# Closing work of layer 0 inside layer 1's first attention block, with moved constants, scattered DMAs and expert groups

## What is computed

```python
xn = _layernorm(x)
x = x + L0_attn(xn) + L0_switchhead(xn)      # softmax attention, and 8 heads with 8 experts each
xn = _layernorm(x)
x = x + L1_attn(xn) + L1_moe(xn)

# L1_attn: positive random features, 16 heads of 8, 64 features
k_prime = ratio * exp(proj k - |k|^2/2 - max over tokens and features) + 1e-4
q_prime = ratio * exp(proj q - |q|^2/2 - max over features) + 1e-4
out = (q_prime @ (k_prime^T v)) / clip(q_prime @ sum(k_prime), 1e-2) @ Wo.T + bo

# L1_moe
logits = xf @ gate_w + gate_b;  top 2 of 8, softmax of the two -> combine
out = sum_e combine_e * (gelu(xf @ w1[e] + b1[e]) @ w2[e] + b2[e]) + gelu(xf @ ws1 + bs1) @ ws2 + bs2
```

## Time and profile before

| | us |
|---|---|
| median of 3 runs | 3363.51 |
| lowest and highest | 3355.54, 3365.3 |
| the profiled execution, its own time | 3354.0 |
| its span in the profile | 3352.2 |

### The profile page before, as it was taken

One profiled execution on the slowest core, in us unless ns is written; L12 is line 12 of the kernel. 1 busy time (PEld: TensorE's weight loads), 2 busy tenths in 40 slices (PEclk: granted clock), 3 DMA queues, 4 the chain that ended last, 5 costly groups with the idle time before them and its releaser, 6 DMA issues. The chain is left out here.

```text
span 3352.2 us, 51674 instructions
## 1 busy us (share of the span) xinstructions
PE 3032.0 (90%) x17486; PEld 2092.8 (62%) x17486; DVE 2384.9 (71%) x4419; ACT 1612.1 (48%) x3262; POOL 1826.2 (54%) x2258
## 2 busy tenths in 40 slices
PE   2999999999999999999999999999999246798967
PEld 1567666666666666666666666666666234566644
DVE  6888888888888888888888888888885330424242
ACT  1355555555555555555555555555555112262612
POOL 1466666666666666666666666666664244011052
PEclk7899999999999999999999999999999577899988
DMA  4000001100100011010101100110000211133211
GB/s 153 20 21 21 21 27 36 31 21 22 34 27 21 21 30 30 22 34 28 32 21 31 30 21 22 34 33 21 21 21 8 50 39 59 61 92 117 64 51 29
DMA packets 143160, 123.47 MB, mean 37 GB/s; under 512 B 28458, under 2 KB 123956, under 8 KB 142900
## 3 DMA queue, kind: packets, MB, share of 16 engines
q1 hardware_dynamic: 130884, 88.88, 9.4%
q0 software_dynamic: 9712, 28.93, 2.8%
q10 hardware_dynamic: 2304, 2.36, 0.4%
HBM read 91.56 MB, written 28.57 MB: 36 GB/s over the span
## 5 line engine op out<-in xcount | busy, mean ns | idle before, releaser
L1167 DVE TENSOR_REDUCE m_peaks<-m_ring 128x1 f32<-128x512 f32 x1024 | 641.5, 682 | 116.9 <-PE m_ring L266 111.2
L925 ACT ACTIVATE m_expA<-m_ring 128x512 f32<-128x512 f32 x1024 | 538.9, 601 | 367.4 <-PE m_sums L354 176.8
L816 POOL TENSOR_TENSOR m_vprod<-m_vprod 128x512 f32<-128x512 f32 x256 | 355.4, 1388 | 497.0 <-DVE m_vprod L1180 495.3
L825 POOL TENSOR_TENSOR m_oprod<-m_oprod 128x512 f32<-128x512 f32 x256 | 328.5, 1283 | 282.3 <-DVE m_oprod L1249 282.3
L317 PE MATMUL m_ring<-m_probT,m_vs 128*128 128x256 f32 x2048 | 466.9, 381 | 0.0
L896 ACT ACTIVATE m_prob<-m_ring,m_negs 128x512 f32<-128x512 f32 x512 | 347.4, 684 | 240.4 <-DVE m_negs L1214 240.4
L317 PEld LDWEIGHTS m_ring<-m_probT,m_vs 128*128 128x128 f32 x2048 | 384.2, 190 | 79.7 <-issue 27.7
L1208 DVE TENSOR_REDUCE m_negs<-m_ring 128x1 f32<-128x512 f32 x512 | 340.6, 685 | 92.4 <-PE m_ring L94 92.0
L1249 DVE TENSOR_TENSOR m_oprod<-m_ring,m_go 128x512 f32<-128x512 f32 x512 | 341.6, 686 | 58.8 <-PE m_ring L94 55.3
L1180 DVE TENSOR_TENSOR m_vprod<-m_ring,m_gate 128x512 f32<-128x512 f32 x512 | 336.9, 684 | 42.0 <-POOL m_vs L818 21.5
L906 ACT ACTIVATE m_probT<-m_ring 128x512 f32<-128x512 f32 x512 | 285.4, 597 | 56.4 <-PE m_ring L305 52.6
(11 more groups left out here) (288 smaller groups left out, 5483.4 us busy)
## 6 DMA issues: line engine op xcount, KB each, us to landing
m_wraw<-in_v_w SPq DMA_DIRECT2D x32, 512.0 KB, 4.0
m_qf<-q_dram SPq DMA_DIRECT2D x128, 128.0 KB, 2.6
m_wraw<-in_o_w SPq DMA_DIRECT2D x32, 512.0 KB, 4.2
q_dram<-m_kf SPq DMA_DIRECT2D x24, 256.0 KB, 3.0
m_xg<-listed SPq DMA_DIRECT2D x39, 128.0 KB
answers<-m_yg SPq DMA_DIRECT2D x39, 128.0 KB, 1.8
listed<-m_oprod SPq DMA_DIRECT2D x9, 512.0 KB, 7.1
sums_dram<-m_sumsT ACTq DMA_DIRECT2D x128, 18.0 KB
```

The source lines that it names most:

```text
L816: vchain(pool.tensor_tensor(vprod[:, 0:512], vprod[:, 0:512], vprod[:, 512:1024], ALU.add))
L825: ochain(pool.tensor_tensor(op[:, 0:512], op[:, 0:512], op[:, 512:1024], ALU.add))
L925: act.activation(expA[hh][:, c * 512:(c + 1) * 512], ring.home["scT", n, k, hh, c][:, :], ACT.Exp)\
L1167: v.tensor_reduce(peaks[:, t, hh, c:c + 1], ring.home["peaks", n, t, hh, c][:, :], AX.X, ALU.max)\
```

## The change

- **Closing of layer 0's last batch.** The products, sums, norm, transposes and routing of batch 3 and the routing of batch 2's last part move out of `layer0` into slots 0 to 13 of block 0 of layer 1. The counting of places moves from slot 1 to slots 13 to 16 in four pieces (`mark_choices`, `keep_places`, `scan_tiles`, `rank_tokens`). SyncE's 33 DMAs of sums and denominators stand at the head of layer 1.
- **Constants.** The 15 loads are issued in layer 0, at step 29 of 32, into memory that layer 0 no longer uses then. The lower parts of the weights are made on VectorE; the parts of x in pieces (ScalarE 512 columns, GpSimd 256).
- **Scattered DMAs.** The rows are sent in slots 16 to 34 (from block 0's end through block 1) instead of 1 to 16; the answers are fetched four at a time in slots 1 to 16 of block 3. In both stretches GpSimd waits for named sums of VectorE (`let_vector`).
- **Groups.** They run in slots 36 to 54 instead of 19 to 53.
- **Units.** Two in block 0, three in block 1, three in block 3. The bias product is four more matmuls at the end of each `output`, into the same tile; `bias` and `add_biases` are gone.

```diff
-UNIT_SLOTS = {2 + 3 * s + part: (s, part) for s in range(4) for part in range(3)}
-FETCH_SLOTS, ANSWER_SLOTS = {1 + 2 * q: q for q in range(8)}, {3 + 2 * q: q for q in range(8)}
+UNIT_SLOTS = {0: {2 + 2 * k: (k // 3, k % 3) for k in range(6)},
+              1: {2 + 5 * s + part: (2 + s, part) for s in range(3) for part in range(3)},
+              B - 1: {2 + 4 * s + part: (5 + s, part) for s in range(3) for part in range(3)}}
+FIRST_SENT, FIRST_GROUP = SLOTS - 2, 2 * SLOTS
+ANSWER_SLOTS = {3 + 2 * q: q for q in range(8)}
...
 # layer0, tensor (the lists of the other engines lose their part in the same way)
-                routing(B - 2)
-                project_out(B - 1, 0)
-                project_out(B - 1, 1)
-                turn_xo(B - 1, 0)
-                turn_xo(B - 1, 1)
-                routing(B - 1)
...
 # layer0, sync
+                    if i == N0 - 3:
+                        sp.wait_ge(xn_turned, 2 * B)
+                        sp.wait_ge(gates_ready, 2 * B)
+                        load_layer1()
...
 def group_slots():
-    first, last = SLOTS + 1, 3 * SLOTS
+    first, last = FIRST_GROUP, 3 * SLOTS + 1
...
 # main1, tensor: output(s)
+                    pe.wait_ge(cT_kept, s + 1)
                     for t in range(4):
                         for k in range(HT):
-                            last = pe.matmul(ps[:, t * P:(t + 1) * P], hT[:, k, t * P:(t + 1) * P], w2[:, k, :],
-                                             start=(k == 0), stop=(k == HT - 1))
+                            pe.matmul(ps[:, t * P:(t + 1) * P], hT[:, k, t * P:(t + 1) * P], w2[:, k, :],
+                                      start=(k == 0), stop=False)
+                        last = pe.matmul(ps[:, t * P:(t + 1) * P], cT[:, t * P:(t + 1) * P], b2, start=False, stop=True)
...
 # main1, tensor: block 0
+                        if b == 0 and u == 5:
+                            project_out(0)
+                            project_out(1)
+                        if b == 0 and u == 9:
+                            turn_xo(0)
+                            turn_xo(1)
+                        if b == 0 and u == 11:
+                            routing(B - 1)
+                        if b == 0 and u == 14:
+                            count_places()
...
 # main1, gpsimd
+                def let_vector(b, u):
+                    s, part = UNIT_SLOTS.get(b, {}).get(u - 1, (None, None))
+                    if part == 2:
+                        pool.wait_ge(x_mixed, s + 1)
+                    if u == 0:
+                        pool.wait_ge(o_divided, 2 * b)
+                    if u == 1:
+                        pool.wait_ge(v_kept, b + 1)
+                    if u == 15:
+                        pool.wait_ge(kvw_made, b + 1)
+                    if u == 16:
+                        pool.wait_ge(o_divided, 2 * b + 1)
...
-                        if b == 0 and 1 <= u < 17:
-                            send_rows(2 * u - 2)
-                            send_rows(2 * u - 1)
-                        if b == 0 and u == 17:
+                        if FIRST_SENT <= n < FIRST_GROUP - 1:
+                            let_vector(b, u)
+                            slots_of = FIRST_GROUP - 1 - FIRST_SENT
+                            for k in range(2 * NT * (n - FIRST_SENT) // slots_of, 2 * NT * (n + 1 - FIRST_SENT) // slots_of):
+                                send_row(k)
+                        if n == FIRST_GROUP - 1:
                             for j in range(NW):
                                 fetch_weights(j)
...
-                        if b == B - 1 and u in FETCH_SLOTS:
-                            fetch_answers(FETCH_SLOTS[u])
+                        if b == B - 1 and 1 <= u < 17:
+                            let_vector(b, u)
+                            fetch_answers((u - 1) // 2, (u - 1) % 2)
```

More of the change, by code:

```diff
@@ L1 @@
+from collections import namedtuple
 from contextlib import ExitStack
+import math
 import numpy as np
@@ L1676, in main1 @@
-        over = early[:, 1536:1536 + NG * EM].rearrange("p (j e) -> p j e", e=EM)
-        full = early[:, 1536 + NG * EM:1536 + NG * EM + 128].rearrange("p (e k) -> p e k", k=16)
+        full = early[:, 768:896].rearrange("p (e k) -> p e k", k=16)
+        scan = [later[:, 384 * k:384 * (k + 1)].rearrange("p (t e) -> p t e", e=EM) for k in range(2)]
+        before = later[:, 768:1024].rearrange("p (t e) -> p t e", e=EM)
+        over = later[:, 0:NG * EM].rearrange("p (j e) -> p j e", e=EM)
+        last_rows = late.oT[:, :].rearrange("p (t d) -> p t d", t=TPB)
@@ L2013, in _ @@
                             project_in(b, 1, qT_made, qT_kept)
-                            turn_combine(b, 0)
-                            if b == 0:
-                                count_places()
-                        s, part = unit_part(b, u)
+                        if b == 0 and u == 0:
+                            routing(B - 2)
+                        s, part = UNIT_SLOTS.get(b, {}).get(u, (None, None))
                         if part == 2:
@@ new lines, in add_late_attn, with token_moments @@
+                def add_late_attn(q):
+                    xt = x[:, NT - TPB + 4 * q:NT - TPB + 4 * q + 4, :].rearrange("p t d -> p (t d)")
+                    v.wait_ge(late.out_made, 2 * B - 1 + q)
+                    v.tensor_tensor(xt, xt, ring.home["late attn", q][:, 0:512], ALU.add).then_inc(late.attn_added, 1)
+                def token_moments():
+                    v.wait_ge(late.attn_added, 2 * B)
+                    for t in range(NT - TPB, NT):
+                        last = v.bn_stats(late.st["bn"][:, t, :], x[:, t, :])
+                    rk(last)
@@ new lines, in choose_experts @@
+                def choose_experts(b):
+                    v.wait_ge(late.lg_kept, b + 1)
+                    one, other = top2(v, rk, late.lg[:, :, :], late.tmp, order[:, :],
+                                      [choice[:, q, b * TPB:(b + 1) * TPB] for q in range(2)])
+                    rk(v.tensor_tensor(one, one, other, ALU.add))
+                    v.tensor_tensor(late.lg[:, :, :], late.lg[:, :, :], spread(late.tmp["first"], 8), ALU.subtract)\
+                        .then_inc(late.lg_ready, 1)
@@ new lines, in mark_choices @@
+                def mark_choices():
+                    v.wait_ge(late.o_divided, 2 * B)
+                    for k in range(2):
+                        v.memset(scan[k][:, 0:16, :], 0.0)
+                        v.memset(cum[k][:, 0:4], 0.0)
+                    for q in range(2):
+                        last = v.tensor_tensor(marks[q], order[:, :].unsqueeze(1).to_broadcast([P, NT, EM]),
+                                               spread(choice[:, q, :], EM), ALU.is_equal)
+                    rk(last)
+                    v.tensor_tensor(marks[2], marks[0], marks[1], ALU.add).then_inc(consts_ready, 1)
@@ L2103, in rank_tokens @@
                                        ALU.add))
+                def rank_tokens():
+                    v.wait_ge(late.mixed, B)
+                    for q in range(2):
+                        rk(v.tensor_tensor(scan[1][:, 16:48, :], combine[:, :, 0:EM], marks[q], ALU.mult))
+                        rk(v.tensor_reduce(shares[:, q, :], scan[1][:, 16:48, :], AX.X, ALU.add))
                     for q in range(2):
@@ L2412, in lower_x, with divide_o @@
                         return
-                    pool.wait_ge(x_upper, b + 1)
-                    lower(pool, xh[b % 2][:, 1, :], xnT[:, b * T:(b + 1) * T], xh[b % 2][:, 0, :]).then_inc(x_split, 1)
+                    for c in range(2):
+                        pool.wait_ge(x_upper, 2 * b + c + 1)
+                        for cols in (slice(512 * c + 256 * k, 512 * c + 256 * (k + 1)) for k in range(2)):
+                            last = lower(pool, xh[b % 2][:, 1, cols], xnT[:, b * T + cols.start:b * T + cols.stop],
+                                         xh[b % 2][:, 0, cols])
+                        last.then_inc(x_split, 1)
+                def divide_o(q):
+                    if q == 0:
+                        pool.wait_ge(late.o_loaded, 512 * B)
+                    heads = slice(8 * q, 8 * q + 8)
+                    pool.tensor_tensor(late.oT[:, :].rearrange("p (u h) -> p h u", h=H0)[:, heads, :], late.o_in[:, heads, :],
+                                       late.rden_in[:, heads, :], ALU.mult).then_inc(late.o_divided, 1)
                 def square_k(b):
```

396 lines of the change are left out of this document (231 added, 165 removed).

## The result

The changed kernel takes 3327.4 us, median of 4 runs (3327.0 to 3332.1); the kernel before took 3363.2, timed beside it. The ratio is 0.990, 95% interval 0.9885 to 0.9914: 36 us less, where I had said 73 less. The profiled execution spans 3330.2 us against 3352.2 before: only 22 less, because it is the slowest of the changed kernel's four, while the one before was 9.5 us under its median.

The account below looks back on a forecast made before the run. Layer 0 is bound by TensorE, so gains lie in the last 750 us, where the bound differs by stage. Terms -64 - 77 + 93 - 24 = -72 us give span 3280, forecast 3290 us, range 3235 to 3347.

Parts of the forecast that it names:

- Start of layer 1, minus 64: Between layer 0 and layer 1: TensorE starts at about 2612 us instead of 2676, bounds minus 61 to minus 65.
- Block 0, 130 us: Block 0 of layer 1: falls from 207 us to 130 with two units and the closing added, minus 77.
- base of 128: Blocks 0 and 3: attention with four units takes 128 us once the visible holes are taken out.
- Rival 4: Block 0: the closing costs more than it hides, plus 20 to 26 us, about 3313; chance 0.11.
- Blocks 1 and 2, unstalled: Blocks 1 and 2 without holes from sends: 121 us for attention with three units, 254 us with the added groups.
- base of 148: Block 2 before the change, taken as 148 us; 16 more groups at 5.6 us each were added to it.
- Rival 3: Block 2: groups become bound by their transfers, slower than before, 3375 us; chance 0.05.
- The sends' holes in block 1, 24 us: Block 1: three bursts of sends cost 8 us each despite the waits, between 0 and 64 us.
- The fetches' holes in block 3, 18 us: Block 3: holes beside the fetches shrink from 35 us to about 18, bounds 0 and 35.
- at most eights: Block 3: after the first 16 fetches run free in slots 1 to 4, later ones come in eights at most.
- rival 1: Blocks 1 and 3: the burst itself is the trouble, 57 us more, about 3347, half 3320; chance 0.2, whole or half.
- the 26 us: Block 0, first burst: a VectorE sum with SBUF and PSUM inputs waits 26 us beside GpSimd's indirect DMAs.

Follow-up runs that it names:

- e7: The kernel before without its 64 sends and 64 fetches (output lacks the experts' part): 3235.0 us, one execution.
- e2: The changed kernel without its 64 sends, 64 fetches and the waits on VectorE's sums: 3240.1 us, ratio 0.966 to the kernel before.
- e4: Separate program, no part of the model: a chain of small TensorE, VectorE and ScalarE steps; 50 steps take 85.0 us alone, 116.4 beside 32 gathers in a row.

## Why the prediction was wrong

I forecast 3290 us and measured 3327.4; as spans of the profiled execution, in which the sum was made, 3280 and 3330.2. By the forecast's own steps, in the order of the sum:

- *Start of layer 1, minus 64: nearly right.* TensorE starts at 2615.20 instead of my 2612. GpSimd's last sum of layer 0 ends at 2612.22, 2.9 us later than before, and from there it takes 3.0, as said. Plus 3 us.

```profile
2611.77 0.45 POOL L864 TENSOR_TENSOR k_x<-k_x,m_oprod 128x128 f32<-128x128 f32 x1
...
2615.20 0.77 PE L98 MATMUL m_ring<-m_xh,m_wh 128*128 128x512 f32 x1 [7.74 <-POOL m_xh L88]
```

- *Block 0, 130 us: right within its bounds.* It took 138.4 (133.7 by the squares, which start 4.7 us after TensorE's first product; here it is counted from that product). Two errors hide each other. My base of 128 for four units is 112 in e7, and the 14 us for closing and ranking are more like 38, if that base holds in block 0 too: 138.4 less 100, which remain of the base when two units at 5 us and the biases' 2 go. That is just inside my bounds of 5 to 40. Rival 4 is right in its direction, by 8 us instead of 20.
- *Blocks 1 and 2, unstalled: near in the sum, block 2 by luck.* Without DMAs block 1 takes 112.8 (I had 121). Block 2 with the groups that spill into block 3's first slot, some 13 us, takes 257 (I had 254). That hides two errors. My base of 148 came from a window that began at 3041 us, 12 us into the block: by the squares block 2 took 162.6 before, with 21 groups, and 37 groups made it 243.7, so 16 more cost 81 us or 5.1 each, not 5.6. Rival 3 (transfers) doesn't appear: the window of block 2 shows TensorE busy 204 of 244 us at 116 GB/s, none of TensorE's waits there is released by `m_wg` or `m_xg`, and the largest, 26 us in all, are for the gelu.
- *The sends' holes in block 1, 24 us: the first step that failed.* The sends cost 41.3 (e2). I had taken three short bursts; they ran in rows of 17, 14 and 17.
- *The fetches' holes in block 3, 18 us: the step that failed most.* The fetches cost 46.5, hardly less than the 48.8 before. I had counted holes of 35 there, because I took everything that was no visible hole for the attention's own time. The base of 128 us was itself stretched by 16 (e7). The argument "at most eights" was wrong as well: the fetches wait for the last group's answers, and the first one starts 17 us into the block. From then on GpSimd is behind its slots and runs in three rows of 16, before it gets down to 8 and 4:

```profile
3168.80 0.99 POOL L2604 DMA_INDIRECT m_rows<-answers,m_place  x1 [15.54 <-DMA answers<-m_yg]
```

Together 87.8 us where I had 42: 46 of the 50 us by which the span missed. The other five terms, the start, block 0, block 1, block 2 and block 3 without their holes, add up to 4 (3 + 8 - 8 + 3 - 2).

So it was rival 1, whose half I had at 3320 and whose whole at 3347: the row itself is the trouble. I gave it 0.2. The two rows on which it rested, TensorE's stepping in the earlier trace rows and the end of the second hole 15 us after the last send, were the right evidence. What I set against it, that VectorE's sums start right behind the last send, fits both theories, since everything starts again there. And one row that spoke plainly against my reading stood in the trace of the kernel before, right above the peaks of the earlier trace rows: the row of sends begins at 2695.53, and ten microseconds into it VectorE runs just such a sum, of x and PSUM (L2227), 2.6 us after its product has ended and 30 us before the row has. What matters is how long the row has been going on, not what VectorE reads:

```profile
2705.42 0.69 DVE L2227 TENSOR_TENSOR k_x<-k_x,m_ring 128x512 f32<-128x512 f32 x1 [5.58 <-remote]
2706.14 2.36 DVE L2154 TENSOR_REDUCE m_peaks<-m_ring 128x16 f32<-128x1024 f32 x2
```

The Trainium skill, SBUF — State Buffer, section "SBUF: two separate sides", is not contradicted after all. By it the unit's sum, which reads one tile of SBUF, should not be blocked, and e4 shows the same standstill with no tile in SBUF read by VectorE. I was wrong to read the 26 us as a trace that disagrees with the rule.

What stays open: what it is in the indirect DMAs that delays TensorE's signals and instructions. Bytes are not it (rows of 128 B cost the same), nor the direction (scatters too), nor, it seems, DMAs of GpSimd as such (32 plain ones, 0.53 us apart, cost nothing; they last 16 us in all, as long as 13 indirect ones, and 12 of those cost 5). The Trainium skill, Runtime: NRT & Kernel Launch, section "Instruction fetch mechanics", says that each engine's instructions are brought in by DMA into a small buffer. Engines that first run on and then get an instruction every 1.40 us would look as if that came late. But the traces list these transfers, as queues of kind "instruction", and they speak against a late refill. In e4, in 85 us of TensorE at full speed (545 to 630), and then in the 26 us in which it steps (648 to 674.5), the queues are:

```profile
q8 instruction: 4, 0.07, 0.3%
q14 instruction: 1, 0.01, 0.0%
...
q0 software_dynamic: 672, 1.38, 17.6%
```

While TensorE steps, no instruction transfer is under way at all. How instructions get on from the buffer no run shows. Another rival is untested: the recording of the profile. In the phase without semaphores the trace holds 19 of the 50 counts of VectorE beside the row, and all 50 without it, so whatever the row holds up, records go missing with it. No run here was timed against the same kernel without recording, so I can't say that the recording has no part in the cost. Open too is why block 3 of the changed kernel, one unit lighter and without its first slot, takes 119 us in e2 where e7's takes 112; the rows show the granted clock at 0.87 against 0.94, and not why it is lower.

And where the 65 us of the earlier start went: without DMAs, from e7 to e2, the start gives 64.8 and block 1 37.5 (its groups left), block 0 takes 10.6 (closing in, two units and the ranking's wait out), block 2 takes 78.4 and block 3 20.6, of which some 13 are groups. That is plus 7 in all. The start less block 0 gives 54, and the groups take 54 (78.4 + 13 - 37.5): by these sums what the overlap of the closing saved was paid for by the groups that now run with nothing of the attention beside them. No run has the closing moved alone.

## What to carry to other kernels

Before a wait on one engine's progress is used to pace another, look at what the engines do that the wait doesn't protect: if all of them stop, and one with all its inputs shows idle time put down to issue, the cause is no operand conflict. Space indirect DMAs on GpSimd in short lots, here four to six with a mean distance of at least 1.5 us, for example by waiting until each four have landed; one pause between long rows doesn't do it, and a wait that is already met is no pause. And measure a block's own time by taking the suspect out once, rather than by subtracting the holes that one sees.

## What the runs showed of the hardware

A GpSimd indirect DMA (128 rows) follows the one before in 1.25 us, and 32 of them in a row hold up a chain through TensorE, VectorE and ScalarE: the first 8 us are free, then a chain with a step of 1.70 us makes four steps in 36 us, as TensorE's signals reach the other two 14 and 24 us late. TensorE, free to run, gets a matmul in 2.80 us instead of 0.22 from the 15th us on, and ScalarE an activation in 1.40 instead of 0.49 from the 22nd; VectorE, free to run, shows no slowing in 30 us. In lots of up to six, at a mean distance of 1.52 us or more, the same 32 cost nothing, and 32 plain DMAs of GpSimd, more than twice as dense, cost nothing either. In the kernel before this was worth 124 us in blocks 0 and 3 and 119 of the whole span of 3352 (e7), and a landed wait after every four gave back 100.
